# Window attention and convolution on one core: a float16 output projection, a copy moved to ScalarE, and statistics spread over more units

## Chip, cores and metric

The kernel runs on one core of a Trainium2 chip. The metric is the time of one execution on the device, in microseconds (us).

## Reference

x is 2 x 128 x 256 x 256 (two batches, 128 channels). The block computes

```
z   = groupnorm(x)                       # 32 groups of 4 channels, eps 1e-5
x1  = x + W_out . attention(z)           # windows of 8x8 queries, 12x12 keys, 4 heads of 32
y   = groupnorm(x1)
y   = y * mask(y)                        # a 32x32 tile is kept if any |value| > 1e-6
out = x1 + conv3x3(y) + bias             # 128 -> 128 channels, zero padding
```

Inside a window a query attends only to the keys whose row and column differences have one parity, so that each window falls into four independent parts of 16 queries and 36 keys. The logits are q.k plus relative logits for height and width, which come from q and two small tables. The second group norm needs the sums over all of x1 of a batch before the convolution of that batch can begin.

## The kernel before

The kernel has three stages, and each engine runs its own instruction stream in each of them; semaphores tie the streams together.

**Stage A** (to 93 us) prepares the weights and gathers the statistics of x of the first batch: VectorE runs `bn_stats` over pieces of 512 elements. A short block, `groupnorm_moments`, turns them into mean and reciprocal deviation.

**Stage B** is a loop over 128 units (`units`, written out in full), a unit being 8 image rows of half the width. `u` is the unit whose scores are computed; other steps belong to units up to 3 ahead or 3 behind. Each unit has four groups (`g`, 512 in all, `n = 4u + g`) of four windows. In a group, TensorE runs in this order: the scores of group n with the relative logits (32 small float32 products, L470), the first transposes of group n-3 (L450), the q and k projections of one part (L432, L437, three float16 products each: high x high, high weight's low half, low x high), the v projections (L484), the attention output of group n-4 (L501, into `ps_o`), the second transposes, and the output projection of a group of unit u-2 (L511, one float32 product of 256 columns into `ps_y`).

VectorE, in order: `brel` (L547), the row sum `ssum` (L551), the copy of the relative logits from `ps_s` to `rel` (L556), the reciprocal (L562), the residual addition `x1` (L571), the score addition (L580), the row maximum (L586), the spreading of q to `qb` (L600). Once a unit each come statistics of x1 (L592, g = 0), maximum and minimum over tiles (L607, g = 1 and 2). In units 6 to 37 four pieces of `bn_stats` of the second batch of x (L531) are spread over the groups.

ScalarE evicts: the transposed probabilities (L638, L656), k (L627), v (L645), the attention output to `of` (L650), then the exponential (L660), the normalisation of rows for a later unit (L684 for edge rows once a unit, L692 for own rows twice) and its float16 high half (L702). GpSimd computes `erel` (L719), the normalised probabilities `d` (L726), the products `prod` of the relative logits with a shift table (L735, waits for `rel`), the subtraction of the maximum (L742) and the low half `zl` (L749). SyncE issues all transfers; the statistics' rows (1 MB a unit, two slots) are queued in the unit that uses them, behind the rows of unit u+3.

At unit 38 the moments of the second batch of x are computed inside the loop: TensorE waits in g = 1 for VectorE's aggregate, and again for five small operations.

**Between B and C** two blocks run with nothing beside them: `groupnorm_moments("gn1", (0, 1))` for both batches of x1, and a block that turns the tile extremes into the tables `ctab` and `dtab` (scale and bias per strip and tile), with a reduction over partitions on GpSimd.

**Stage C** first writes two rows of zeros to `x1` in memory (`zrow`), loads x1 strips of 8 rows, normalises them on ScalarE (L911), combines rows on GpSimd (L984), splits into high (ScalarE, L919) and low half (VectorE, L966), multiplies on TensorE (L892) and adds on VectorE (L956), over 64 strips.

Of the kernel before, what the change touches and what calls it, by code (L numbers as in the profile page):

```python
# [5 lines left out]
F32 = mybir.dt.float32  # L6
# [74 lines left out]
def conv_preact_program(nc, x_in, wqkv_in, wout_in, rel_in, wconv_in, bias_in, ident_in, gsum_in,  # L81
                        shift_in, edge_in, own_head_in, x1_dram, out):
    with ExitStack() as ctx:
# [5 lines left out]
        wo = sb("wo", C, F32)  # L89
# [49 lines left out]
        def moments_tables(dve, link, batches, sqrt_done):  # L139
# [9 lines left out]
            for b in batches:  # L149
                link(dve.tensor_copy(mean_t[:, b * hs:(b + 1) * hs], view(moments, 0, 128, 2 * b, [[0, hs]])))  # L150
                link(dve.tensor_copy(rstd_t[:, STRIPS + b * hs:STRIPS + (b + 1) * hs],
                                     view(gn[5], 0, 128, b, [[0, hs]])))
            lo, hi = batches[0] * hs, (batches[-1] + 1) * hs
# [4 lines left out]
            for part in range(3):  # L158
                cols = slice(part * STRIPS + lo, part * STRIPS + hi)
                link(dve.scalar_tensor_tensor(shift_t[:, cols], rstd_t[:, cols], -1.0, mean_t[:, lo:hi],  # L160
                                              ALU.mult, ALU.mult))

# [45 lines left out]
        with ExitStack() as pa:  # L208
# [16 lines left out]
            with nc.Block() as block:  # L225
# [26 lines left out]
                def _(dve):  # L252
# [22 lines left out]
                    dve.tensor_copy(wo[:], rawn[:, SPANS[1][0]:SPANS[1][1]])  # L275
                    dve.tensor_copy(wq_h[:], rawn[:, 0:3 * C]).then_inc(w_qh, 1)
                    dve.wait_ge(w_qh, 1)
# [39 lines left out]
        with ExitStack() as pb:  # L317
            names = ("zf_done", "zh_done", "zl_done", "q_mm", "k_mm", "kf_done", "qb_done", "s_mm", "rel_out", "prod_done",
                     "b_done", "e_done", "s2_done", "max_done", "sub_done", "exp_done", "sum_done", "rcp_done",
                     "norm_done", "t_mm", "pt0_done", "pt1_done", "v_mm", "vf_done", "o_mm", "of_done", "y_mm",  # L320
                     "x1_done", "x1_read", "x1_stored", "zeroed", "st_used", "gn_agg_done", "gn_sum_done", "gn_step_done",
                     "gn_sqrt_done")
# [3 lines left out]
            st_loaded = [pb.enter_context(nc.semaphore(f"b_st_loaded{h}")) for h in range(2)]  # L326
            STW = WS * W
            st = sb("st", 2 * STW, F32, pb)
# [14 lines left out]
            of = sb("of", 2 * 1024, F32, pb)  # L343
# [14 lines left out]
            FIRST, LOOP = 6, 4  # L358
            STRIPS_1 = STRIPS // B
            EARLY = STRIPS_1 // LOOP  # L360
            GN = FIRST + LOOP * EARLY
            GT = UNITS * GROUPS

            GROUP_STEPS = 2 + 5

            def units(eng, body):

                some = lambda v, top: 0 <= v < top
                for u in range(-3, UNITS + 4):
                    body(u, u // 2, u % 4, some,  # L370
                         (u - FIRST, (u - FIRST) // 2) if FIRST <= u < GN else None, u == GN)

# [9 lines left out]
            def _(sp):  # L382
                def body(u, s, slot, on, stat, moments_due):
# [9 lines left out]
                    if stat is not None:  # L393

                        row = settled(sp, (stat[0] + STRIPS_1) * WS + PAD)
                        sp.wait_ge(sem["st_used"], (stat[0] + 1) * PAR)
                        sp.dma_start(st[:, h * STW:(h + 1) * STW],
                                     x_in[:, bass.ds(row, WS), :].rearrange("p a b -> p (a b)")
                                     ).then_inc(st_loaded[h], 16)
# [6 lines left out]
                    if on(u - 1, UNITS):  # L406
# [8 lines left out]
                                          UW * r:UW * r + UW]).then_inc(xr_loaded[r], 16)  # L415
                units(sp, body)
                sp.wait_ge(sem["x1_stored"], UNITS * 16)

            @block.tensor
            def _(pe):  # L420
                def project(n, p, slot, u, moments_due):
# [4 lines left out]
                    if moments_due:  # L426
                        pe.wait_ge(sem["gn_agg_done"], 1)
                        pe.matmul(ps_q[:, 0:2], gsum[:], aggr[:, 2:4], start=True, stop=True
                                  ).then_inc(sem["gn_sum_done"], 1)
                        pe.wait_ge(sem["gn_step_done"], GROUP_STEPS)  # L430
# [22 lines left out]
                def body(u, s, slot, on, stat, moments_due):  # L453
                    for g in range(GROUPS):
# [20 lines left out]
                        if on(u + ahead, UNITS):  # L475
                            project(n, (g + 1) % PAR, slot + ahead, u + ahead, moments_due and g == 1)
# [11 lines left out]
                        if on(n - 4, GT):  # L488
# [4 lines left out]
                            need(pe, sem["of_done"], m)  # L493
# [537 lines left out]
```

## Time and profile before

| | us |
|---|---|
| median of 3 runs | 3701.91 (3698.52 to 3707.66) |
| the profiled execution, its own time | 3702.19 |
| its span, first to last instruction | 3700.40 |
| PE (TensorE matmul) busy | 3491.4 |
| DVE (VectorE) busy | 3349.1 |
| ACT (ScalarE) busy | 2966.0 |
| POOL (GpSimd) busy | 2575.1 |

The span is what the trace shows; the profiled execution's own time is 1.79 us more, which lies around the first and the last instruction. A busy share over the whole span mixes three stages with different limits, so the rows below are taken by stage. Rows of the timeline give start and duration; the time from one start to the next (the step) is shorter than the duration where neighbours overlap.

### The profile page before, as it was taken

The numbers are of one execution on the slowest core, as the hardware profiler recorded it, in microseconds if no ns is written. First come the engines' busy times: TensorE is split into PE (matmuls) and PEld (weight loads), VectorE is DVE, ScalarE is ACT, GpSimd is POOL, SyncE is SP. The second block draws the span as 40 slices with busy tenths as digits, with TensorE's granted clock in tenths as the row PEclk, the third lists the DMA queues.
The fourth block names the chain that finished last, engine by engine and source line by source line (L and its number), as shares of the span: only waits on it lengthen the run. The fifth ranks groups of instructions, "written<-read, shape, count | busy, mean of one in ns | idle before, by whom it ended". The sixth has DMA issues, their size and how long they took to land. (4 is left out here: it accounts for less than half of the span.)

```text
span 3700.4 us, 127356 instructions
## 1 busy us (share of the span) xinstructions
PE 3491.4 (94%) x51718; PEld 2480.6 (67%) x51718; DVE 3349.1 (91%) x5626; ACT 2966.0 (80%) x5320; POOL 2575.1 (70%) x3344
## 2 busy tenths in 40 slices
PE   0799999998999999999999999999589999999999
PEld 0587777777888888888888888888434444444444
DVE  9699999999999999999999999999789888888887
ACT  0788888887999999999999999998377777777774
POOL 1677777776777777777777777777366666666664
PEclk9999999999999999999999999999799999999999
DMA  8244544443333333333333333333244434344332
GB/s 374 79 132 133 159 134 154 148 139 105 103 103 97 94 98 103 103 97 91 101 103 103 95 91 103 103 100 83 69 160 162 154 146 154 147 154 154 154 154 83
DMA packets 492549, 464.06 MB, mean 125 GB/s; under 512 B 9664, under 2 KB 469312, under 8 KB 469440
## 3 DMA queue, kind: packets, MB, share of 16 engines
q1 hardware_dynamic: 491968, 455.92, 38.4%
q8 instruction: 412, 6.75, 0.8%
q14 instruction: 169, 1.38, 0.1%
HBM read 321.40 MB, written 134.48 MB: 123 GB/s over the span
## 5 line engine op out<-in xcount | busy, mean ns | idle before, releaser
L984 POOL TENSOR_TENSOR sb_tf<-sb_cf 128x1024 f32<-128x1024 f32 x256 | 609.4, 2382 | 392.2 <-DVE sb_tl L966 370.3
L450 PE MATMUL ps_t<-sb_ident,sb_d 128*108 128x128 f32 x4096 | 662.3, 284 | 6.2 <-ACT sb_pt L638 1.9
L600 DVE TENSOR_TENSOR sb_qb<-ps_q,sb_own_head 128x1024 f32<-128x1024 f32 x512 | 621.1, 1213 | 14.9 <-PE ps_q L432 14.9
L470 PEld LDWEIGHTS ps_s<-sb_kf,sb_qb 128*64 128x64 f32 x16384 | 519.1, 138 | 171.5 <-issue 162.9
L719 POOL TENSOR_TENSOR sb_erel<-sb_brel 128x288 f32<-128x288 f32 x512 | 351.5, 686 | 395.6 <-DVE sb_brel L547 394.7
L892 PE MATMUL ps_c<-sb_th,sb_wc_h 128*128 128x512 f16 x1536 | 584.3, 380 | 40.3 <-DVE sb_tl L966 40.2
L470 PE MATMUL ps_s<-sb_kf,sb_qb 128*64 128x54 f32 x16384 | 585.6, 224 | 2.4 <-DVE sb_scores L580 2.4
L892 PE MATMUL ps_c<-sb_th,sb_wc_l 128*128 128x512 f16 x1536 | 583.3, 380 | 0.0
L892 PE MATMUL ps_c<-sb_tl,sb_wc_h 128*128 128x512 f16 x1536 | 583.2, 380 | 0.0
L749 POOL TENSOR_TENSOR sb_zl<-sb_zf,sb_zh 128x396 f16<-128x396 f32 x512 | 481.1, 940 | 83.1 <-ACT sb_zh L702 83.1
L735 POOL TENSOR_TENSOR sb_prod<-sb_rel,sb_shift 128x192 f32<-128x192 f32 x1024 | 502.1, 511 | 0.0
L919 ACT CAST sb_th<-sb_tf 128x1024 f16<-128x1024 f32 x256 | 263.9, 1043 | 258.9 <-POOL sb_tf L984 258.9
L450 PEld LDWEIGHTS ps_t<-sb_ident,sb_d 128*108 128x108 f32 x4096 | 410.6, 131 | 87.8 <-ACT sb_pt L638 12.1
L726 POOL TENSOR_TENSOR sb_d<-sb_scores,sb_srcp 128x288 f32<-128x288 f32 x512 | 342.6, 669 | 160.3 <-DVE sb_srcp L562 160.3
L966 DVE TENSOR_TENSOR sb_tl<-sb_tf,sb_th 128x1024 f16<-128x1024 f32 x256 | 420.0, 1641 | 20.4 <-ACT sb_th L919 20.3
L956 DVE SCALAR_TENSOR_TENSOR sb_oc<-ps_c,sb_wscale,sb_oc 128x1024 f32<-128x1024 f32 x256 | 322.6, 1281 | 86.2 <-PE ps_c L892 86.1
L911 ACT ACTIVATE sb_cf<-sb_xc,sb_dtab,sb_ctab 128x32 f32<-128x32 f32 (+2 forms) x768 | 357.2, 551 | 26.4 <-DMA sb_xc<-x 26.4
L484 PE MATMUL ps_v<-sb_wq_h,sb_zh 128*108 128x128 f16 x2048 | 369.9, 219 | 0.0
L484 PE MATMUL ps_v<-sb_wq_l,sb_zh 128*108 128x128 f16 x2048 | 369.9, 219 | 0.0
L484 PE MATMUL ps_v<-sb_wq_h,sb_zl 128*108 128x128 f16 x2048 | 369.9, 219 | 0.0
L627 ACT COPY sb_kf<-ps_k 128x576 f32<-128x576 f32 x512 | 331.6, 648 | 43.0 <-PE ps_k L437 42.7
L656 ACT COPY sb_pt<-ps_t 108x512 f32<-108x512 f32 x512 | 302.1, 590 | 75.7 <-PE ps_t L450 71.7
(117 smaller groups left out, 8228.0 us busy)
## 6 DMA issues: line engine op xcount, KB each, us to landing
sb_xb<-rows SPq DMA_DIRECT2D x128, 780.0 KB, 6.5
sb_xc<-x SPq DMA_DIRECT2D x64, 1280.0 KB, 5.4
sb_x<-rows SPq DMA_DIRECT2D x128, 512.0 KB, 4.1
x<-sb_x SPq DMA_DIRECT2D x128, 512.0 KB, 3.3
out<-sb_oc SPq DMA_DIRECT2D x64, 1024.0 KB, 3.9
sb_abuf<-rows SPq DMA_DIRECT2D x16, 2048.0 KB, 11.7
sb_st<-rows SPq DMA_DIRECT2D x32, 1024.0 KB, 9.3
sb_raw<-wconv SPq DMA_DIRECT2D x1, 576.0 KB, 3.7
```

Source lines behind the costliest of these rows:

```text
L450: last = pe.transpose(ps_t[0:KV, wj * 128:(wj + 1) * 128], d[:, at:at + KV], ident[:])
L470: last = pe.matmul(s_at, qb[:, qc:qc + QB], kf[:, kc:kc + KR], start=True, stop=True)
L484: last = pe.matmul(ps_v[0:KV, p * C:(p + 1) * C], z_at(z, vslot, p, GW * WK * vg, [[1, KV]]), w[:, 2 * C:3 * C], start=(c == 0), stop=(c = ...
L600: dve.tensor_tensor(view(qb, 0, 128, vh * QBW + p * NW * QB, [[QB, NW], [QN, HEADS], [1, QN]]), view(ps_q, 0, 128, 0, [[QN, NW], [0, HEADS ...
L719: pool.tensor_tensor(view(erel, 0, 128, 0, [[KN, PAIRS], [KS, KS], [1, KS]]), view(brel, 0, 128, 0, [[KS, PAIRS], [0, KS], [1, KS]]), view ...
L726: pool.tensor_tensor(view(d, 0, 128, b0 * DB, [[DSLOT, PAIRS], [1, KN]]), view(sp_, 0, 128, b0 * NS, [[KN, PAIRS], [1, KN]]), view(srcp, 0 ...
L735: last = pool.tensor_tensor(view(prod, 0, 128, ax * PAIRS * KS * QS, [[KS * QS, PAIRS], [QS, KS], [1, QS]]), view(rel, 0, 128, b0 * PAIRS ...
L749: pool.tensor_tensor(z_at(zl, vslot, p, 0, [[1, PLANE]]), view(zf, 0, 128, (vslot % 2) * PAR * PLANE + p * PLANE, [[1, PLANE]]), z_at(zh, ...
L892: last = pe.matmul(m_at, wt[:, tap], t_at(z), start=(c == 0), stop=(c == 8))
L911: last = act.activation(view(cf, 0, 128, c0 + off, dims), view(xc, 0, 128, r + off, dims), ACT.Identity, bias=dtab[:, col], scale=ctab[:, ...
L966: dve.tensor_tensor(view(tl, 0, 128, at, [[CW, PAIRROWS], [1, W]]), view(tf, 0, 128, k * TF, [[W, PAIRROWS], [1, W]]), view(th, 0, 128, at ...
L984: pool.tensor_tensor(tf[:, k * TF:(k + 1) * TF], view(cf, 0, 128, c0 + ra * W, [[2 * W, PAIRROWS], [1, W]]), view(cf, 0, 128, c0 + rb * W, ...
```

## The change

- The output projection takes `wo_h`, `wo_l` (float16 halves of the weight) and `oh`, `ol` (float16 halves of the attention output): three float16 products instead of one float32. ScalarE writes `oh` instead of `of`; VectorE writes `ol` = `ps_o` - `oh`, behind its residual addition of the group. TensorE's next attention output waits for `ol`.
- The copy of the relative logits moves from VectorE to ScalarE, behind the first transposed copy.
- The statistics of the second batch of x are taken in half strips (two pieces each): two half strips in each of units 0 to 3, one in each of units 4 to 59, all in g = 3. Four slots; the load is issued a unit ahead, last in SyncE's order.
- The moments of the second batch of x move from unit 38 to unit 60. The moments of x1 of the first batch are computed in the loop at unit 70, its tile extremes, the reduction and its tables at unit 71. For the second batch of x1 they move into the block of stage C, where ScalarE waits for the tables only at the strip where batch two begins. The zero rows are written in the loop.

```diff
-        wo = sb("wo", C, F32)
+        wo_h, wo_l = sb("wo_h", C, F16), sb("wo_l", C, F16)
...
+            def gathered(u):
+
+                if 0 <= u < DOUBLE:
+                    return (2 * u, 2 * u + 1)
+                return (u + DOUBLE,) if DOUBLE <= u < HALVES - DOUBLE else ()
+
+            MOMENTS = {HALVES - DOUBLE: 1, UNITS // B + 6: 0}
+            MASK = UNITS // B + 7
...
+                    for k in gathered(u + 1):
+
+                        row, r = H + k * (WS // 2) + PAD, k % ST
+                        if k >= ST:
+                            sp.wait_ge(sem["st_used"], 2 * (k - ST + 1))
+                        sp.dma_start(st[:, r * HALF:(r + 1) * HALF],
+                                     x_in[:, row:row + WS // 2, :].rearrange("p a b -> p (a b)")
+                                     ).then_inc(st_loaded[r], 16)
...
-                            need(pe, sem["of_done"], m)
+                            need(pe, sem["ol_done"], m)
...
-                            pe.matmul(ps_y[:, 0:QP], wo[:], of[:, ob * 1024 + g * QP:ob * 1024 + (g + 1) * QP],
-                                      start=True, stop=True).then_inc(sem["y_mm"], 1)
+                            for c, (o, w) in enumerate(((oh, wo_h), (oh, wo_l), (ol, wo_h))):
+                                last = pe.matmul(ps_y[:, 0:QP], w[:], o[:, ob * 1024 + g * QP:ob * 1024 + (g + 1) * QP],
+                                                 start=(c == 0), stop=(c == 2))
+                            last.then_inc(sem["y_mm"], 1)
...
-                        if on(n, GT):
-                            dve.wait_ge(sem["s_mm"], n + 1)
-                            need(dve, sem["prod_done"], n - 1)
-                            dve.tensor_copy(view(rel, 0, 128, b0 * PAIRS * 2 * RN, [[2 * RN, PAIRS], [1, 2 * RN]]),
-                                            view(ps_s[g % 2], 0, 128, KN, [[KR, PAIRS], [1, 2 * RN]])
-                                            ).then_inc(sem["rel_out"], 1)
...
+                        if on(n - 5, GT):
+
+                            v, vslot, vg = (u - 1, slot - 1, g - 1) if g else (u - 2, slot - 2, GROUPS - 1)
+                            dims = [[QP, PAR], [1, GW * QN]]
+                            dve.wait_ge(sem["oh_done"], n - 4)
+                            need(dve, sem["y_mm"], (v - 1) * PAR)
+                            dve.tensor_tensor(view(ol, 0, 128, (vslot % 2) * 1024 + vg * GW * QN, dims),
+                                              view(ps_o, 0, 128, 0, [[GW * QN, PAR], [1, GW * QN]]),
+                                              view(oh, 0, 128, (vslot % 2) * 1024 + vg * GW * QN, dims), ALU.subtract
+                                              ).then_inc(sem["ol_done"], 1)
...
+                        if g == 3:
+                            for k in gathered(u):
+                                r = k % ST
+                                dve.wait_ge(st_loaded[r], (k // ST + 1) * 16)
+                                for c in range(2):
+                                    at = UNITS * 6 + (2 * k + c) * 6
+                                    dve.bn_stats(stats[:, at:at + 6],
+                                                 st[:, r * HALF + c * 512:r * HALF + (c + 1) * 512]
+                                                 ).then_inc(sem["st_used"], 1)
+                        if u in MOMENTS:
+                            b = MOMENTS[u]
+                            if g == 0:
+                                moments_sums(dve, link[b], (b,), gn_sem[b]["agg_done"])
+                            if g == 2:
+                                moments_tables(dve, link[b], (b,), gn_sem[b]["sqrt_done"], edges=(b == 1))
+                        if u == MASK and g == 0:
+                            tile_extremes(dve, link[0], 0)
+                            dve.tensor_copy(ext[1][:, 0:1], ext[0][:, 0:1]).then_inc(sem["tiles_done"], 1)
+                        if u == MASK and g == 2:
+                            row_tables(dve, link[0], 0, sem["all_tiles"])
...
+                        if on(n, GT):
+                            act.wait_ge(sem["s_mm"], n + 1)
+                            need(act, sem["prod_done"], n - 1)
+                            act.copy(view(rel, 0, 128, b0 * PAIRS * 2 * RN, [[2 * RN, PAIRS], [1, 2 * RN]]),
+                                            view(ps_s[g % 2], 0, 128, KN, [[KR, PAIRS], [1, 2 * RN]])
+                                            ).then_inc(sem["rel_out"], 1)
...
-        groupnorm_moments("gn1", (0, 1))
...
+                    if j + 2 == CSTRIPS // B:
+                        act.wait_ge(sem["step_done"], TABLE_STEPS)
...
+                link = linker(dve, sem["step_done"])
+                moments_sums(dve, link, (1,), sem["agg_done"])
...
+                moments_group(dve, link, (1,), ps_c, sem["sum_done"])
+                moments_tables(dve, link, (1,), sem["sqrt_done"], edges=False)
+                tile_extremes(dve, link, 1)
+                dve.tensor_copy(ext[1][:, 0:1], ext[0][:, 0:1]).then_inc(sem["tiles_done"], 1)
+                row_tables(dve, link, 1, sem["all_tiles"])
```

`tile_extremes` and `row_tables` hold the work of the old block between B and C, for one batch. `row_tables` takes threshold and scale in one operation and four copies where the old block had eight scalings.

## Rows read from the trace of the kernel before

**Rows 1.** Windows: span, then busy us and instructions by engine, clock, DMA share

```profile
240.00:880.00 640.00, 619.84 (x11639) 499.71 (x11638) 619.74 (x1262) 543.24 (x1043) 481.46 (x757) 1.00 0.46 143
...
945.00:2567.00 1622.00, 1622.00 (x30923) 1331.10 (x30920) 1505.82 (x3025) 1466.81 (x2775) 1280.05 (x2016) 1.00 0.36 99
```

**Rows 2.** Timeline (start, duration) of ScalarE: edge rows, once a unit

```profile
247.98 1.48 ACT L684 ACTIVATE sb_zf<-sb_xb,sb_shift_t,sb_rstd_t 128x260 f32<-128x260 f32 x2
...
877.60 1.46 ACT L684 ACTIVATE sb_zf<-sb_xb,sb_shift_t,sb_rstd_t 128x260 f32<-128x260 f32 x2
...
945.09 1.50 ACT L684 ACTIVATE sb_zf<-sb_xb,sb_shift_t,sb_rstd_t 128x260 f32<-128x260 f32 x2
...
2566.99 1.50 ACT L684 ACTIVATE sb_zf<-sb_xb,sb_shift_t,sb_rstd_t 128x260 f32<-128x260 f32 x2
```

**Rows 3.** Waits from 240 to 860 us: total, times, longest

```profile
DVE sb_stats L531 <- DMA sb_st<-rows: 15.0, 27, 1.6
```

**Rows 4.** Timeline of TensorE's matmuls, late in the loop

```profile
1701.74 0.60 PE L511 MATMUL ps_y<-sb_of,sb_wo 128*128 128x256 f32 x2
1702.27 1.14 PE L470 MATMUL ps_s<-sb_kf,sb_qb 128*64 128x54 f32 x32
...
1703.82 0.30 PE L432 MATMUL ps_q<-sb_zh,sb_wq_h 128*128 128x256 f16 x1
...
1704.23 0.33 PE L437 MATMUL ps_k<-sb_zh,sb_wq_h 128*128 128x396 f16 x1
...
1705.35 0.22 PE L484 MATMUL ps_v<-sb_wq_h,sb_zl 128*108 128x128 f16 x1
1705.50 0.65 PE L501 MATMUL ps_o<-sb_pt,sb_vf 108*32 108x64 f32 x32
```

**Rows 5.** Timeline of VectorE: early stage, late stage, end of the loop

```profile
405.26 0.44 DVE L551 TENSOR_REDUCE sb_ssum<-sb_scores 128x8 f32<-128x288 f32 x1
405.62 0.30 DVE L556 COPY sb_rel<-ps_s 128x144 f32<-128x144 f32 x1
405.83 0.20 DVE L562 RECIPROCAL sb_srcp<-sb_ssum 128x8 f32<-128x8 f32 x1
...
409.40 0.68 DVE L531 BATCH_NORM_STATS2 sb_stats<-sb_st 128x6 f32<-128x512 f32 x1
...
1703.79 0.43 DVE L571 SCALAR_TENSOR_TENSOR sb_x<-ps_y,sb_oscale,sb_x 128x256 f32<-128x256 f32 x1
...
2625.24 0.45 DVE L551 TENSOR_REDUCE sb_ssum<-sb_scores 128x8 f32<-128x288 f32 x1 [0.76 <-ACT sb_scores L660]
2625.73 0.20 DVE L562 RECIPROCAL sb_srcp<-sb_ssum 128x8 f32<-128x8 f32 x1
```

**Rows 6.** Timeline of ScalarE: copy of the attention output

```profile
1706.22 0.37 ACT L650 COPY sb_of<-ps_o 128x256 f32<-128x256 f32 x1
```

**Rows 7.** Timeline between B and C; chain that ended last (its last three)

```profile
2646.73 7.28 DVE L118 BATCH_NORM_AGGREGATE sb_aggr<-sb_stats 128x2 f32<-128x768 f32 x2 [0.33 <-PEq L317]
...
2656.07 0.20 ACT L197 ACTIVATE sb_gn<-sb_gn 128x2 f32<-128x2 f32 x1 [8.09 <-DVE sb_gn L137]
...
2660.64 1.29 DVE L783 TENSOR_REDUCE sb_tile_ext<-sb_tmax 128x64 f32<-128x256 f32 x2 [0.56 <-PEq L180]
...
2667.60 0.23 DVE L794 TENSOR_SCALAR sb_tile_abs<-sb_tile_abs 128x128 f32<-128x128 f32 x1 [2.60 <-POOL sb_tile_abs L819]
...
2677.20 5.43 DMA sb_xc<-x
...
2682.66 6.70 ACT sb_cf L911 x16
...
2716.39 978.35 PE ps_c L892 x4518
```

**Rows 8.** Timeline of VectorE in stage C: the low half, twice

```profile
2729.43 1.30 DVE L966 TENSOR_TENSOR sb_tl<-sb_tf,sb_th 128x1024 f16<-128x1024 f32 x1
...
2760.87 2.47 DVE L966 TENSOR_TENSOR sb_tl<-sb_tf,sb_th 128x1024 f16<-128x1024 f32 x1
```

More of the change, by code:

```diff
@@ L152, in moments_tables @@
                                      view(gn[5], 0, 128, b, [[0, hs]])))
+            if not edges:
+                return
             lo, hi = batches[0] * hs, (batches[-1] + 1) * hs
@@ L161, in moments_tables, with tiles_of @@
                                               ALU.mult, ALU.mult))
+        ctab = sb("ctab", 3 * CSTRIPS * TC, F32)
+        dtab = sb("dtab", 3 * CSTRIPS * TC, F32)
+        nmean = sb("nmean", B, F32)
+        TR = ROWS // TILE
+        SPT = TILE // CROWS
+        ext = [sb(f"tile_ext{j}", TR * TC, F32) for j in range(2)]
+        tabs = sb("tile_abs", TR * TC, F32)
+        zrow = sb("zrow", W, F32)
+        def tiles_of(t, b):
+            return t[:, b * TR // B * TC:(b + 1) * TR // B * TC]
@@ new lines, in tile_extremes @@
+        def tile_extremes(dve, link, b):
+            hs, n = STRIPS // B, TR // B
+            for t, dst, op in ((tmax, ext[0], ALU.max), (tmin, ext[1], ALU.min)):
+                for h in range(2):
+                    link(dve.tensor_reduce(view(dst, 0, 128, b * n * TC + 4 * h, [[TC, n], [1, 4]]),
+                                           view(t, 0, 128, b * n * 8 * SPT + 4 * h, [[8 * SPT, n], [1, 4], [8, SPT]]),
+                                           AX.X, op))
+                part = tiles_of(dst, b)
+                link(dve.tensor_scalar(part, part, mean_t[:, b * hs:b * hs + 1],
+                                       rstd_t[:, STRIPS + b * hs:STRIPS + b * hs + 1], ALU.subtract, ALU.mult))
+            link(dve.scalar_tensor_tensor(tiles_of(ext[0], b), tiles_of(ext[1], b), -1.0, tiles_of(ext[0], b),
+                                          ALU.mult, ALU.max))
@@ L425, in project @@
                     need(pe, sem["qb_done"], piece)
[L426 to L430, printed above, removed]
+                    if due is not None:
+                        pe.wait_ge(gn_sem[due]["agg_done"], 1)
+                        pe.matmul(ps_q[:, 0:2], gsum[:], aggr[:, 2 * due:2 * due + 2], start=True, stop=True
+                                  ).then_inc(gn_sem[due]["sum_done"], 1)
+                        pe.wait_ge(gn_sem[due]["step_done"], GROUP_STEPS)
                     for c, (z, w) in enumerate(PRODUCTS):
@@ L475, in body @@
                         if on(u + ahead, UNITS):
-                            project(n, (g + 1) % PAR, slot + ahead, u + ahead, moments_due and g == 1)
+                            project(n, (g + 1) % PAR, slot + ahead, u + ahead, MOMENTS.get(u) if g == 1 else None)
                         if on(n - 3, GT):
@@ L522, in _, with body @@
                 last.then_inc(sem["zeroed"], 1)
[L523 to L535 removed]
+                link = [linker(dve, gn_sem[b]["step_done"]) for b in range(B)]
+                def body(u, s, slot, on):
                     h = slot % 2
@@ L877, in _ @@
             def _(pe):
+                pe.wait_ge(sem["agg_done"], 1)
+                pe.matmul(ps_c[:, 0:2], gsum[:], aggr[:, 2:4], start=True, stop=True).then_inc(sem["sum_done"], 1)
                 def body(j, t, slot, on):
```

186 lines of the change are left out of this document (70 added, 116 removed).

## Prediction

> **What bounds the kernel now.** I read three views in this order: the windows, the timeline of each engine, and the chain of waits at the two stage boundaries. The windows [rows 1] split the unit loop in two. From 945 us on TensorE is busy in all 1622.00 us, VectorE in 1505.82 (93%), ScalarE in 1466.81 (90%), GpSimd in 1280.05. From 240 to 880 us, while the statistics of the second batch are gathered, VectorE has 619.74 of 640 us (97%) and TensorE waits. The period of a unit is read between starts of the edge-row activation of ScalarE, one pair per unit [rows 2]: 84 periods from 945.09 to 2566.99 make 19.31 us each; 31 from 247.98 to 877.60 make 20.31. So a late unit is set by TensorE; an early one by VectorE, whose work in it is 619.74 / 640 x 20.31 = 19.67 us, and most of the rest is a wait for the statistics' rows, 15.0 us in 27 waits [rows 3], 0.48 us per unit. VectorE's work in a late unit is 1505.82 / 1622 x 19.31 = 17.93 us, ScalarE's 17.46.
>
> From 877.60 to 945.09 three units take 67.49 us, 9.56 more than three of 19.31 [rows 2]: that is the computing of one batch's moments inside the loop. Behind the loop the convolution can't begin: its first normalisation on ScalarE starts at 2682.66, while the moments block began at 2646.73 [rows 7]. From 2716.39 the end chain is TensorE alone for 978.35 us [rows 7].
>
> **The change, part by part.**
>
> *1. Output projection on TensorE.* Today one float32 product goes from 1701.74 to the start of the scores at 1702.27: 0.53 us [rows 4]. Three float16 products of the same 128x256 shape stand in the same trace as the q projection: they begin at 1703.82 and the k products follow at 1704.23, so 0.137 us each [rows 4]. What follows a float16 product with float32 weights shows at the v products: the last one starts at 1705.35, the attention product at 1705.50 [rows 4]. A 512-column product of the convolution takes 978.35 / 4518 = 0.217 us [rows 7], so 128 columns take 0.054, 256 take 0.108, and some 0.10 of the 0.15 is the turn. The new block: two steps of 0.137, then 0.108 of columns and 0.10 = 0.48. It saves 0.05 us a group, 0.21 a unit: the floor of TensorE falls from 19.31 to 19.10. Bounds: nothing saved (19.31), or no turn at all, 3 x 0.137 = 0.41, 0.12 saved (18.83). I take 0.05, put together from this engine's own steps.
>
> *2. The copy of the relative logits leaves VectorE.* Step from its start to the next instruction: 405.62 to 405.83, 0.21 us [rows 5]. But it now stands between the sum (405.26, step 0.36) and the reciprocal (405.83), which waits for that sum. Where no copy stands between them, at the loop's end, the sum starts at 2625.24 and the reciprocal at 2625.73 [rows 5]: 0.49. So 0.36 + 0.21 = 0.57 becomes 0.49: only 0.08 us is gained.
>
> *3. The low half of the attention output comes to VectorE.* 128x256, one operand from PSUM and one from SBUF. The nearest row is the residual addition of the same size and places, which lasts 0.43 us [rows 5]; neighbours overlap by 0.08 (the sum lasts 0.44 and its step is 0.36), so its step is 0.35. Bounds: 0.21, the copy's step, and the whole 0.43. I take 0.35. With part 2 that is +0.27 a group, +1.08 a unit.
>
> *4. Statistics.* Now four 512-element pieces in each of 32 units; then two in each of 56 units (units 4 to 59) and four in units 0 to 3. A piece costs its duration of 0.68 less the overlap of 0.08: 0.60 [rows 5]. So VectorE has in a unit with two pieces 19.67 - 1.20 + 1.08 = 19.55 in the figures of the early stage, and in one without pieces 19.67 - 2.40 + 1.08 = 18.35. Adding up single steps instead gives about 0.1 more, because a busy share hides short gaps; I take 19.65 and 18.45. The waits for rows go, since four slots are loaded a unit ahead. In SyncE's order these loads now come last in their unit, behind the store of x1 and the residual's rows; behind their own wait stand the rows of a unit three ahead, which have time. The two transfers of zeros join that queue once, at unit 4, at no cost. The rest of the old gap, 20.31 - 19.67 - 0.48 = 0.16 a unit, I keep as 0.14: 19.79. VectorE thus stays the bound for 56 units, 0.69 above the new floor, and is no longer it behind them.
>
> *5. The copy on ScalarE.* The copy of 256 columns from PSUM takes 0.37 us [rows 6]; 144 columns take an estimated 0.28, a step of 0.19, so 0.76 a unit: 17.46 becomes 18.2 of 19.1. The added wait, for the scores' products, is met already: the transposed copy ahead of it waits for later products of TensorE. Queued behind the copy are the k and v evictions and the attention output, and TensorE waits for those a group later; GpSimd's product waits for it too. The 0.9 us a unit that is left covers it; without that cover it would cost up to 0.76 a unit, 95 us in 125 units. TensorE's attention product of the next group now waits for the low half instead of the copy. In the late stage VectorE does that half behind the residual addition of the group, at 1703.79 + 0.35 [rows 5], so till about 1704.6, and the product comes at 1705.50 [rows 4]: it hides too. In the early stage it makes TensorE follow VectorE, which is the bound there anyway.
>
> *6. Moments of the finished x1, first batch, at unit 70.* The same code as the stall of 9.56 us, so +9.6; from zero, if covered, to 12.
>
> *7. Tile extremes and tables of the first batch at unit 71.* Both batches' extremes ran from 2660.64 to 2665.00, and the reduction over partitions added 2.60 before 2667.60 [rows 7]. Half the extremes is an estimated 2.6 us, the reduction is partly waited for, and the tables cost an estimated 2.3 (some ten operations of 0.1 to 0.5 us, as the one at 2667.60 of 0.23). With 0.6 us a unit of room on VectorE I take 5, between 0 and 10.
>
> *8. The boundary.* The new block starts at once with the second batch's moments while the rows load. The aggregate of two batches lasted 7.28 [rows 7]; one takes 3.64. The old ScalarE square root began at 2656.07, 9.34 us after the block's start; less 3.64 that is 2646.73 + 5.70, with its own 0.2 it is 2652.6, and two small fills make it 2652.9. The rows need 5.43 us from their issue, which now can be at about 2647.1 [rows 7]: 2652.5. So the normalisation starts at 2652.9 and not 2682.66: 29.8 earlier. VectorE is first needed an estimated 10 us behind it, after the first strip of 6.70 us and GpSimd's first rows [rows 7]; its own small work (tables of the moments, 2.6 of extremes, 2.6 of reduction, 2.3 of row tables) ends by my count at about 2663, just in time. I take 29; bounds 24 and 30. The 64 strips themselves don't change.
>
> *9. Setup:* one subtraction and a wait more on VectorE, +0.6.
>
> **The sum.** Loop: floor 125 units x 0.21 = -26; 56 units x 0.69 = +38.6 in place of the old early excess, 31 x 1.00 = 31 us; units 0 to 3 with their double load +2.8; the first moments stall stays; the new one +9.6; tables +5. That is -1.0. Tail of the loop an estimated -0.5, boundary -29, setup +0.6: -30. The profiled execution took 3702.19 us (span 3700.40, 1.79 around it), 0.28 above the median of 3701.91. So 3702.2 - 30 = 3672, ratio 0.992; against the median the same within a microsecond.
>
> **The rivals.**
>
> A. *Statistics spread so thin that TensorE sets the early units too.* If the low half costs 0.21 and the waits vanish, VectorE needs 19.65 - 0.56 = 19.1: -38.6, 3633. Against it: the nearest row says 0.35. Chance 0.10.
>
> B. *The float16 block saves nothing.* The turn between number formats takes back 0.05. Only the 68 or so units that TensorE sets lose: +14, 3686. Chance 0.12.
>
> C. *The copy on ScalarE delays GpSimd.* It now comes behind a transposed copy in ScalarE's order and not straight behind the scores, so GpSimd's product, its subtraction and the exponential on ScalarE form a ring with ScalarE's own work. GpSimd has 4.1 us a unit free (1280.05 of 1622.00, [rows 1]), which speaks against it. If the ring is longer than a group in one group of four by 0.2 us, 125 units lose 25: 3697. Chance 0.10.
>
> D. *The boundary gain is lost* to another wait (rows, or VectorE's small work under GpSimd's float32 work): +29, 3701. Chance 0.03.
>
> E. *Slower than before: the low half on VectorE is drawn out by GpSimd.* In the convolution the same kind of subtraction takes 1.30 us at one time and 2.47 at another [rows 8], a factor of 1.9. At 0.35 x 1.9 = 0.67 the early units cost 1.28 more (+72) and the late ones come to 19.7, 0.6 above the floor (+43): 3787. It decides from a step of about 0.48 us on: +0.13 x 4 x 56 = 29. For it speaks that GpSimd is busy in 79% of the loop [rows 1]; against it that the residual addition, which also reads PSUM and SBUF, lasts 0.43 [rows 5] beside the same GpSimd work. Chance 0.05. The Trainium skill (GPSIMD Engine Reference, Specifications) says that contention strikes VectorE instructions with two SBUF inputs or in a 2-port mode; by that rule this subtraction, with one SBUF input, is spared, and the rows agree.
>
> **How the numbers follow.** My forecast has 0.60, the rivals 0.10, 0.12, 0.10, 0.03 and 0.05. Its own range, from the bounds of parts 1, 3, 6, 7 and 8 taken together, is 3654 to 3692. The range of 3645 to 3700 leaves out A's full gain, the upper part of C, D and E. What this measurement can tell from no change is 0.3%, 11 us: faster is below 3691. Faster: 0.58 + 0.10 + 0.10 + 0.02 = 0.80. Same: 0.02 + 0.02 + 0.07 + 0.03 = 0.14. Slower: 0.06, which is E and the upper end of C.
>
> **What the profile after would show.** Period of late units 19.10 (right), 19.31 (B), more (E or C). Periods of units 4 to 59 near 19.8, VectorE without gaps; 19.1 would be A. The low half's duration: 0.43 right, above 0.56 is E. Two units with some 10 us more, at 60 and 70, and one with 5. First normalisation some 6 us behind the end of the loop. The prediction is wrong if ScalarE stops waiting for TensorE in the late stage, or if TensorE waits for the low half there.

## The result and the profile after

The changed kernel takes 3675.62 us (median of 4 runs, 3671.46 to 3676.63); the kernel before, on the same chip, 3702.09 (4 runs). The ratio is 0.9925, 95% interval 0.9911 to 0.9940: faster by 0.75%, some 4 us above the forecast of 3672. The profiled execution spans 3673.7 us, 26.7 less than before.

Windows of the changed kernel, in the columns of [rows 1] (span; busy time of TensorE, its weight loads, VectorE, ScalarE and GpSimd; granted clock, DMA share, GB/s), from an early and a late part of the loop without stalls:

```profile
240.00:880.00 640.00, 631.43 (x12184) 520.75 (x12183) 630.56 (x1246) 588.68 (x1213) 497.65 (x787) 1.00 0.42 123
1600.00:2550.00 950.00, 946.88 (x18638) 792.08 (x18640) 909.41 (x1804) 892.36 (x1855) 761.50 (x1201) 1.00 0.37 101
```

VectorE is busy in 98.5% of the early window, TensorE in 99.7% of the late one: the bounds lie where the prediction put them. The starts of the edge rows, as in [rows 2]:

```profile
112.99 1.45 ACT L768 ACTIVATE sb_zf<-sb_xb,sb_shift_t,sb_rstd_t 128x260 f32<-128x260 f32 x2
...
213.15 1.48 ACT L768 ACTIVATE sb_zf<-sb_xb,sb_shift_t,sb_rstd_t 128x260 f32<-128x260 f32 x2
...
1288.02 1.49 ACT L768 ACTIVATE sb_zf<-sb_xb,sb_shift_t,sb_rstd_t 128x260 f32<-128x260 f32 x2
1317.66 1.45 ACT L768 ACTIVATE sb_zf<-sb_xb,sb_shift_t,sb_rstd_t 128x260 f32<-128x260 f32 x2
1340.59 1.48 ACT L768 ACTIVATE sb_zf<-sb_xb,sb_shift_t,sb_rstd_t 128x260 f32<-128x260 f32 x2
...
1493.82 1.48 ACT L768 ACTIVATE sb_zf<-sb_xb,sb_shift_t,sb_rstd_t 128x260 f32<-128x260 f32 x2
1522.36 1.46 ACT L768 ACTIVATE sb_zf<-sb_xb,sb_shift_t,sb_rstd_t 128x260 f32<-128x260 f32 x2
1554.90 1.49 ACT L768 ACTIVATE sb_zf<-sb_xb,sb_shift_t,sb_rstd_t 128x260 f32<-128x260 f32 x2
...
2561.37 1.48 ACT L768 ACTIVATE sb_zf<-sb_xb,sb_shift_t,sb_rstd_t 128x260 f32<-128x260 f32 x2
```

From 213.15 to 1288.02 there are 55 periods of 19.54 us on average; the usual one is 19.52. The usual late period is 18.89. In between are two stalls: 29.64 and 22.93 (and 19.89, 18.88, 20.03 behind them) around unit 60, together 16.9 over five times 18.89; and 28.54 and 32.54 (then 19.85) at units 70 and 71, together 24.3 over three times 18.89. The forecast had 24.2 for all of them, the trace has 41.2. From the row at 112.99 to 2561.37 the loop takes 2448.38 us. Before, the same row stood here:

```profile
112.48 1.46 ACT L684 ACTIVATE sb_zf<-sb_xb,sb_shift_t,sb_rstd_t 128x260 f32<-128x260 f32 x2
```

and to 2566.99 [rows 2] it was 2454.51: -6.1.

TensorE and VectorE in a late group, answering to [rows 4] and [rows 5]:

```profile
2102.75 0.30 PE L497 MATMUL ps_q<-sb_zh,sb_wq_h 128*128 128x256 f16 x1
2102.89 0.30 PE L497 MATMUL ps_q<-sb_zh,sb_wq_l 128*128 128x256 f16 x1
...
2103.16 0.33 PE L502 MATMUL ps_k<-sb_zh,sb_wq_h 128*128 128x396 f16 x1
2103.33 0.33 PE L502 MATMUL ps_k<-sb_zh,sb_wq_l 128*128 128x396 f16 x1
...
2105.49 0.27 PE L577 MATMUL ps_y<-sb_oh,sb_wo_h 128*128 128x256 f16 x1
2105.60 0.27 PE L577 MATMUL ps_y<-sb_oh,sb_wo_l 128*128 128x256 f16 x1
2105.71 0.27 PE L577 MATMUL ps_y<-sb_ol,sb_wo_h 128*128 128x256 f16 x1
2105.92 0.27 PE L535 MATMUL ps_s<-sb_kf,sb_qb 128*64 128x54 f32 x2
```

```profile
2102.36 0.44 DVE L609 TENSOR_REDUCE sb_ssum<-sb_scores 128x8 f32<-128x288 f32 x1
2102.84 0.20 DVE L614 RECIPROCAL sb_srcp<-sb_ssum 128x8 f32<-128x8 f32 x1
2102.96 0.43 DVE L623 SCALAR_TENSOR_TENSOR sb_x<-ps_y,sb_oscale,sb_x 128x256 f32<-128x256 f32 x1
2103.31 0.42 DVE L636 TENSOR_TENSOR sb_ol<-ps_o,sb_oh 128x256 f16<-128x256 f32 x1
2103.64 0.45 DVE L643 TENSOR_TENSOR sb_scores<-ps_s,sb_erel 128x288 f32<-128x288 f32 x1
```

The projection block now takes 2105.49 to 2105.92, 0.43 us in place of 0.53. The sum stands 0.48 ahead of its reciprocal (predicted 0.49), and the low half lasts 0.42 with a step of 0.33 (predicted 0.43 and 0.35).

The timeline between the loop and the convolution, answering to [rows 7] (start, duration, engine; in brackets the idle time ahead and what ended it):

```profile
2642.13 3.62 DVE L118 BATCH_NORM_AGGREGATE sb_aggr<-sb_stats 128x2 f32<-128x768 f32 x1 [0.33 <-PEq L367]
...
2647.80 0.20 ACT L957 ACTIVATE sb_gn<-sb_gn 128x1 f32<-128x1 f32 x1 [4.41 <-DVE sb_gn L137]
2647.90 6.68 ACT L932 ACTIVATE sb_cf<-sb_xc,sb_dtab,sb_ctab 128x32 f32<-128x32 f32 x16
...
2653.02 0.55 POOL L1004 PARTITION_ALL_REDUCE sb_tile_abs<-sb_tile_ext  x1 [28.61 <-DVE sb_tile_ext L969]
...
2655.04 0.75 DVE L208 TENSOR_SCALAR sb_dtab<-sb_ctab,sb_nmean 128x768 f32<-128x768 f32 x1
2662.36 7.94 POOL L1015 TENSOR_TENSOR sb_tf<-sb_cf 128x1024 f32<-128x1024 f32 x3 [8.80 <-issue]
```

The normalisation starts 5.8 us behind the block's start at 2642.13; the forecast was 6.2 (2646.73 to 2652.9). But the first strip is complete at 2654.58, VectorE's tables at 2655.8 (13.7 behind the block's start, where 16.3 was forecast), and GpSimd's first subtraction waits until 2662.36, for nothing that the profile shows. From the block's start to the end of the last addition on VectorE the kernel takes 1027.24 us; before, 3696.05 - 2646.73 = 1049.3. That gains 22, not 29. In the kernel before, a gap behind the reduction could not show: GpSimd had nothing to do until ScalarE's first strip.

```profile
2666.77 0.72 POOL L819 PARTITION_ALL_REDUCE sb_tile_abs<-sb_tile_ext  x1 [36.85 <-issue]
2689.44 25.81 POOL L984 TENSOR_TENSOR sb_tf<-sb_cf 128x1024 f32<-128x1024 f32 x9 [21.94 <-ACT sb_cf L911]
```

The same gap stands in the loop, at unit 71 (GpSimd's timeline, then VectorE's):

```profile
1537.98 0.54 POOL L839 PARTITION_ALL_REDUCE sb_tile_abs<-sb_tile_ext  x1 [5.82 <-PE ps_t L515]
1545.45 0.68 POOL L803 TENSOR_TENSOR sb_erel<-sb_brel 128x288 f32<-128x288 f32 x1 [6.93 <-issue]
```

```profile
1546.16 0.46 DVE L643 TENSOR_TENSOR sb_scores<-ps_s,sb_erel 128x288 f32<-128x288 f32 x1 [9.82 <-POOL sb_erel L803]
```

So the difference of 26.7 is: setup +0.5, loop -6.1, its tail +1.0, behind the loop -22.1.

### The profile page after: what moved, and what is told of

Read it like the earlier page. It is cut to its first block and busy times, and to the rows that moved or that the text cites. A ratio compares the mean times of both kernels' runs of the same rounds, so it can differ in the third digit from the quotient of the medians.

```text
span 3673.7 us, 129440 instructions
## 1 busy us (share of the span) xinstructions
PE 3461.0 (94%) x52232; PEld 2490.3 (68%) x52232; DVE 3399.8 (93%) x5647; ACT 3035.0 (83%) x5835; POOL 2570.7 (70%) x3345
## 5 line engine op out<-in xcount | busy, mean ns | idle before, releaser
L566 PE MATMUL ps_o<-sb_pt,sb_vf 108*32 108x64 f32 x16384 | 339.6, 222 | 29.6 <-DVE sb_ol L636 13.9
```

The source lines that it names most:

```text
L566: last = pe.matmul(o_at, v_at, p_at, start=True, stop=True)
```

## The experiments

All times are medians against the kernel before, run on the same chip; in brackets the ratio to it and its 95% interval. "Period" is the time between the starts of the edge rows. "Theory 1" is the first explanation that an expectation names. The code shown is cut down to what matters.

**One part alone, and one undone.** First the float16 projection and its low half put into the kernel before, nothing else:

```diff
-pe.matmul(ps_y[:, 0:QP], wo[:], of[...], start=True, stop=True)
+for c, (o, w) in enumerate(((oh, wo_h), (oh, wo_l), (ol, wo_h))):
+    last = pe.matmul(ps_y[:, 0:QP], w[:], o[...], start=(c == 0), stop=(c == 2))
+dve.tensor_tensor(ol[...], ps_o[...], oh[...], ALU.subtract)   # behind the residual addition
```

> The kernel before with the float16 projection and its low half on VectorE alone. Theory 1 (the step costs VectorE 0.33 a group and TensorE gains 0.10): a late unit has 17.93 + 4 x 0.33 = 19.25 us of VectorE work against a TensorE floor of 18.89, so VectorE sets it at about 19.3, no gain over 19.31; the 32 units with statistics go from 20.31 to 21.6, +42. Sum: 3745 us, slower by 1.2%. Rival (TensorE's gain of 0.42 a unit reaches the time, since neighbours on VectorE overlap more when it is pressed): late units 19.0, 90 x -0.3 = -27, sum about 3717.

Measured: 3700.42 us (0.9993, 0.9983 to 1.0002). Late units fall to 18.88, though VectorE carries both the copy and the low half; units with four pieces of statistics rise from 20.31 to 21.04. My sum of 19.25 for a late unit was too high, and with it both forecasts, 3745 and the rival's 3717: it added a step of 0.33 to a busy share of 17.93. From 2000 to 2370 us VectorE is busy in 98.7% of the time (365.20 of 370) and TensorE in all of it, so it is still TensorE that sets these units, as the rival had it. 84 late periods gain 33 us, 31 early ones lose 25 and the stall 2: nearly nothing is left.

The copy of the relative logits moved alone:

```diff
-dve.tensor_copy(view(rel, ...), view(ps_s[g % 2], ...))      # between sum and reciprocal
+act.copy(view(rel, ...), view(ps_s[g % 2], ...))             # behind the transposed copy
```

> The kernel before with the copy of the relative logits on ScalarE alone. Theory 1 (VectorE gains only 0.08 us a group, because the reciprocal must then wait for its own sum): units with statistics 20.31 - 0.3 = 20.0, 32 x -0.3 = -10; late units stay 19.31. Sum 3692 us. Rival (the whole step of 0.21 is gained): -27, 3675. Rival (GpSimd is delayed by the copy's place behind ScalarE's transposed copy): late units above 19.31, time at or above 3702.

Measured: 3699.6 us (0.9992, 0.9982 to 1.0002). 29 periods from unit 8 average 20.05 in place of 20.34, late ones are 19.31 as before. GpSimd does not lengthen a unit. The early periods bear theory 1 out (0.29 gained, 0.3 forecast). The time gained 3 us of the 10 forecast: 0.08% can't be told from no change.

The statistics spread alone, with the boundary left as it was:

```diff
-if stat is not None: stat_pieces(stat, h, (0, 4, 1, 2)[g], (1, 0, 1, 2)[g])   # units 6 to 37
+if g == 3:
+    for k in gathered(u): ...                                # two pieces a unit, units 4 to 59
```

> The kernel before with the statistics spread over 60 units and loaded a unit ahead, the moments at unit 60, and nothing else. Theory 1 (VectorE's work per unit is what set the early units): 17.93 + 1.20 = 19.13, under TensorE's 19.31, so all units take 19.31 and the 31 us of the old early excess go: 3671 us, as low as the whole change. Rival (part of the excess was the short order around the pieces, which stays): early units at 19.5, 56 x 0.2 = 11 more, 3682.

Measured: 3672.35 us (0.9914, 0.9898 to 0.9931), the same as the whole change. Its periods are 19.31 from unit 5 to the end, but for one stall of 28.73 (and 18.78 behind it).

The changed kernel with its float32 projection back:

```diff
-for c, (o, w) in enumerate(((oh, wo_h), (oh, wo_l), (ol, wo_h))): ...
-dve.tensor_tensor(ol[...], ps_o[...], oh[...], ALU.subtract)
+pe.matmul(ps_y[:, 0:QP], wo[:], of[...], start=True, stop=True)
```

> The changed kernel with the float32 projection put back and no low half on VectorE. Theory 1: late units 19.31 again in place of 18.89, 68 x 0.42 = +29; early units 19.31 in place of 19.52, 56 x -0.21 = -12; the first stall falls from 16.9 to about 10, since the attention product no longer waits for VectorE: -7. Sum 3686 us, 0.3% above the changed kernel. Rival (the late gain of 0.42 came from the copy that left VectorE and not from the block of products): late units stay 18.9, early 18.9, time about 3650.

Measured: 3671.2 us (0.9912, 0.9896 to 0.9929). All units take 19.31; the stalls at 60 and 70 cost 8.27 each and the one at 71 12.8. So late units follow the block of products, as theory 1 has it, but its sum of 3686 is 15 us too high. Outside the stalls 57 late periods make 24 us, less 4.5 in odd ones of the changed kernel, where I had 29; the early units and the stalls give back 24 where I had 19. Inside the whole change the float16 projection is worth nothing that can be measured (the intervals of 0.9912 and 0.9925 overlap).

The changed kernel with the copy back on VectorE:

```diff
-act.copy(view(rel, ...), view(ps_s[g % 2], ...))
+dve.tensor_copy(view(rel, ...), view(ps_s[g % 2], ...))      # between sum and reciprocal
```

> The changed kernel with the copy of the relative logits back on VectorE. Theory 1 (its place between the sum and the reciprocal makes it cost only 0.07 to 0.08 us there): early units 19.52 + 0.3 = 19.8, 56 x 0.3 = +17; late units stay 18.89; 3692 us. Rival (it costs its whole step of 0.21): early units 20.36, +47, 3723, and late units above 18.89.

Measured: 3688.03 us (0.9965, 0.9951 to 0.9979). Early units take 19.85, 0.33 more or 0.08 a group; late ones 18.89. Where VectorE is the bound the copy costs what stood in the prediction.

**What bounds an early unit.** The statistics of the second batch left out, its moments taken from other columns:

```diff
 def gathered(u):
-    if 0 <= u < DOUBLE: ...
+    return ()
```

> The changed kernel without loading and gathering the second batch's statistics in the loop; its moments are worked out from other columns, so the second batch's values are wrong by that. Theory 1 (two pieces of statistics a unit are what holds the early units at 19.52): all early units at 18.89, 56 x -0.63 = -35, and 3641 us. Rival (TensorE's wait for the low half holds them, with or without statistics): early units stay above 19.2, over 3655.

Measured: 3635.39 us (0.9817, 0.9800 to 0.9833): early units at 18.89.

The two pieces of a unit in groups 1 and 3:

```diff
-if g == 3: both pieces of the unit
+return ((u + DOUBLE, g // 2),) if g in (1, 3) and ... else ()   # one piece in a group
```

> The changed kernel with the two statistics pieces of a unit in two groups (1 and 3) and not both in group 3; nothing else. Theory 1 (the sum of VectorE's work in a unit sets the early units, 98.5% of 19.52): at most the idle 0.29 goes, 19.25 to 19.5, between -15 and 0: 3661 to 3676 us. Rival (the two pieces in one group of 4.7 us are what TensorE waits for, and the sum is not the bound): early units at 18.9 to 19.1, 3645 us.

Measured: 3675.28 us (0.9925, 0.9908 to 0.9942), early units at 19.51 to 19.52. The place of the pieces changes nothing; the sum of VectorE's work is the bound, and the last 1.5% of the window is no room here. The periods of the kernels bound by VectorE also give the prices: four pieces, copy and low half 21.04; two pieces, 19.85; two without the copy, 19.52. A piece is thus (21.04 - 19.85) / 2 = 0.595, and an early unit without pieces would ask 19.52 - 1.19 = 18.33 of VectorE, under TensorE's 18.89.

**The reduction over partitions.** A plain copy in its place leaves out the maximum over channels:

```diff
-pool.partition_all_reduce(tiles_of(tabs, b), tiles_of(ext[0], b), 128, RMAX)
+pool.tensor_copy(tiles_of(tabs, b), tiles_of(ext[0], b))
```

> The changed kernel with both reductions over partitions on GpSimd replaced by a plain GpSimd copy of the same tile; it leaves out the maximum over channels. Theory 1 (after a reduction GpSimd takes some 7 to 9 us before its next instruction, and that gap, not the reduction's own 0.55 us, holds up the loop at unit 71 and the start of the convolution): unit 71 falls from 32.5 by about 8, to 24 or 25; the first GpSimd subtraction of the convolution comes straight behind the first normalised strip, about 7 us earlier. Sum 3676 - 15 = 3661 us. Rival (VectorE's own small work sets both places): both stay, at most -1 each, 3674.

Measured: 3656.97 us (0.9878, 0.9862 to 0.9895), 18.6 less than the changed kernel and 4 under theory 1. Unit 71 falls from 32.54 to 22.75, and from the block's start to the end it is 1019.34 us in place of 1027.24. GpSimd's timeline at both places:

```profile
1533.13 0.24 POOL L839 COPY sb_tile_abs<-sb_tile_ext 128x64 f32<-128x64 f32 x1 [2.47 <-DVE sb_tile_ext L690]
1533.61 0.69 POOL L803 TENSOR_TENSOR sb_erel<-sb_brel 128x288 f32<-128x288 f32 x1 [0.24 <-DVE sb_brel L605]
...
2641.76 0.24 POOL L1004 COPY sb_tile_abs<-sb_tile_ext 128x64 f32<-128x64 f32 x1 [28.66 <-DVE sb_tile_ext L969]
2643.50 8.12 POOL L1015 TENSOR_TENSOR sb_tf<-sb_cf 128x1024 f32<-128x1024 f32 x3 [1.50 <-ACT sb_cf L932]
```

Behind a copy the next instruction follows at once, or with the strip that it waits for. The gap belongs to the reduction.

**Versions built on this.** The maximum over channels serves only to tell whether any channel exceeds a threshold. A 0/1 map multiplied by a matrix of ones says the same, exactly, on TensorE:

```diff
+dve.tensor_scalar(ext1, ext0, THRESHOLD, None, ALU.is_gt)
+pe.matmul(ps_q[:, QP:QP + TN], ones[:], ext1, start=True, stop=True)
+dve.tensor_scalar(tabs, ps_q[:, QP:QP + TN], 0.5, rstd, ALU.is_gt, ALU.mult)  # ahead of the eviction of q
+if g in SLOTS(u): steps.emit(dve, 1)       # one queued small instruction a unit, from 66 on
```

> The changed kernel, whole computation, with the first batch's moments and tables not done in two units but one small VectorE instruction in each unit from 66 to 123, TensorE reading and writing a free part of the query accumulator, the maximum over channels taken as a product of a 0/1 map with ones on TensorE (so no GpSimd reduction), and seven eighths of the second aggregate ahead of the boundary. Theory 1: the stalls at units 70 and 71 (9.7 + 13.7 = 23.4) go but for 1 or 2, and the convolution starts 7 earlier: 3676 - 22 - 7 = 3647 us. Rival (VectorE has no room in a late unit, and the same work costs the same spread thin): some 18 us of it come back, 3665.

Measured: 3641.15 us (0.9831, 0.9815 to 0.9847). The edge rows at units 68 to 72, where the changed kernel has its second pair of stalls:

```profile
1470.43 1.48 ACT L889 ACTIVATE sb_zf<-sb_xb,sb_shift_t,sb_rstd_t 128x260 f32<-128x260 f32 x2
...
1545.95 1.49 ACT L889 ACTIVATE sb_zf<-sb_xb,sb_shift_t,sb_rstd_t 128x260 f32<-128x260 f32 x2
```

18.88 in all four periods: the same work, one instruction a unit, fits into VectorE's spare time. From the block's start to the end it is 1019.97, -7.3, as with the plain copy:

```profile
2624.92 0.69 PE L1014 MATMUL ps_c<-sb_tile_ext,sb_ones 128*128 128x64 f32 x2 [6.20 <-DVE sb_tile_ext L257]
2625.65 0.28 DVE L267 TENSOR_SCALAR sb_tile_abs<-ps_c,sb_rstd_t 128x64 f32<-128x64 f32 x1 [0.78 <-PE ps_c L1014]
...
2629.87 7.93 POOL L1133 TENSOR_TENSOR sb_tf<-sb_cf 128x1024 f32<-128x1024 f32 x3 [30.71 <-ACT sb_cf L1052]
```

Then each projection where its engine has room:

```diff
+terms = ((oh, wo_h), (oh, wo_l), (ol, wo_h)) if u - 2 >= 42 else ((of, wo),)
+GATHER = {0: (0, 1), ..., 4: (8,), 5: (9, 10), ...}          # three pieces a unit, done at unit 41
```

> The kernel e8_thin_tables with the float32 projection in the first 42 strips' units, where statistics are gathered three pieces a unit, and the float16 projection from unit 42 on; both batches' moments spread thin. Theory 1 (VectorE sets a unit that has both statistics and the low half; TensorE sets all others): units 4 to 42 at 19.31, units 44 to 127 at 18.89, no stall at 60, 70 or 71: the loop is 2380 us long in place of 2448, with the boundary 3676 - 68 - 7 = 3601 us. Rival (three pieces a unit are too many beside the float32 projection): units 4 to 42 at 19.7, 3617. Rival (the low half costs the same in late units once the small work is added): late units at 19.0 to 19.1, 3615.

Measured: 3608.61 us (0.9748, 0.9731 to 0.9764), the best of all, 2.5% under the kernel before. Edge rows:

```profile
210.37 1.49 ACT L899 ACTIVATE sb_zf<-sb_xb,sb_shift_t,sb_rstd_t 128x260 f32<-128x260 f32 x2
...
866.95 1.49 ACT L899 ACTIVATE sb_zf<-sb_xb,sb_shift_t,sb_rstd_t 128x260 f32<-128x260 f32 x2
...
2501.29 1.49 ACT L899 ACTIVATE sb_zf<-sb_xb,sb_shift_t,sb_rstd_t 128x260 f32<-128x260 f32 x2
```

34 early periods of 19.31; behind unit 60 the usual one is 18.88. From unit 43 to 58, with two small instructions a unit, it is 19.06. There, from 1180 to 1260 us, VectorE is busy in 78.83 of 80 us and TensorE in 79.64. I take it that VectorE's room is used up; no run tests it. These units make 3 of the 7.6 us over the forecast, and odd periods the rest.

Two attempts to bring the early units to 18.9 as well:

```diff
-dve.tensor_reduce(brel, prod[..., 4], AX.X, ALU.add)
+pool.tensor_tensor(halfsum, prod[..., 0:2], prod[..., 2:4], ALU.add)   # units 0 to 42
+pool.tensor_tensor(brel, halfsum[..., 0], halfsum[..., 1], ALU.add)
```

> The kernel e9_mixed with the float16 projection in all units, and in the first 43 units the sum over four neighbours of the relative products done by two additions on GpSimd in place of VectorE's reduction; the computation is whole. Theory 1 (GpSimd has the room: 15.1 us a unit and an estimated 3.1 more, under 18.89; VectorE falls to an estimated 18.3): all units at 18.9, 39 x -0.42 = -16 against e9_mixed, 3592 us. Rival (the longer chain on GpSimd, from ScalarE's copy to the scores, becomes the bound of a group): early units at 19.5 or more, 3616 us or above.

Measured: 3620.42 us (0.9780, 0.9764 to 0.9797). The periods alternate, 18.96 with two pieces and 19.74 with four in group 3; 30 from unit 8 average 19.40. From 240 to 880 us TensorE waits 16 times for the low half, 12.5 us in all, and VectorE 90 times for GpSimd's `erel`, 25.1 us. Theory 1's 3592 is missed by 28, and the time is the rival's (3616 or above).

```diff
-at = pieces of whole halves, all in group 3
+at = divmod(q, 4) if q < 16 else ((q - 16) // 3 + 4, (q - 16) % 3 + 1)   # unit, group of piece q
```

> The kernel e10_pool_sums with one statistics piece in each of the groups 1, 2 and 3 of units 4 to 41, in place of two or four pieces in group 3. Theory 1 (the alternation of 18.96 and 19.74 there comes from the four pieces in one group): all early units at 18.95 to 19.05, 38 x -0.35 = -13, 3607 us, the same as e9_mixed within 0.1%. Rival (GpSimd, busy in 95% of these units, holds them at 19.3): 3619 us.

Measured: 3617.74 us (0.9770, 0.9754 to 0.9786). The alternation is gone, most early periods are 19.05 to 19.20, but several reach 19.6 to 20.9, and 30 periods from unit 8 average 19.35. The place of the pieces explains the alternation: TensorE's waits for the low half fall to 2.4 us. The time is that of the rival, in which GpSimd holds the early units (3619). GpSimd is busy in 610.05 of 640 us there, and VectorE waits 63 times for its `erel`, 21.5 us in all, a wait that the changed kernel's early window does not have; TensorE's waits without a cause in the profile are 6.8 us. No run separates the two, so what holds these units above 18.9 stays open. Both lose to e9_mixed.

## Why the prediction was right, and where it was off

The likeliest case came true, with the time inside its own range and 4 us above it; that closeness owes something to errors of opposite sign.

*1, the projection.* The saving is 0.10 to 0.11 a group, close to the 0.12 of the bound that I had called "no turn at all", and the floor is 18.89, not 19.10. The cost behind the last product is there, though: 2105.71 to 2105.92, 0.21, as I had put it (0.108 + 0.10). What was wrong is the step: I took 0.137 from the products of q, whose moving operand is read in pieces of four, and those still step by 0.14 in the trace after; the ones of the projection, with contiguous columns, step by 0.11. The products of k, contiguous too, step by 0.17 for 396 columns, the same 0.43 ns a column, against 0.54 for q. No run changed the layout of one product alone. 60 late units x 0.21 = -13 us against the forecast.

*2 and 3, the copy and the low half.* Both right: 0.08 a group (e11_rel_back) and a step of 0.33.

*4, the early units.* The mechanism is right (e7_no_stats, e12_apart), and the piece costs 0.595 where 0.60 was predicted. The size was 19.52, not 19.79: my addition in the figures of the busy share gave 19.55, and I then laid 0.10 for "single steps" and 0.14 for an old gap on top. Neither exists once the rows come in time. 55 x -0.27 = -15 us.

*5, the copy on ScalarE,* hides: the late units take 18.89 with it (changed kernel) and without (e11_rel_back), early ones gain. GpSimd waits for it often (114.5 us in 152 waits from 1600 to 2550 us), at no cost to the period. Neither sign by which the prediction would have been wrong is there: in that window ScalarE still waits for TensorE's transposes (35.7 us in 106 waits), and TensorE never for the low half.

*6, the moments.* The second stall, at unit 70, is 28.54 - 18.89 = 9.65, as predicted. The first was taken as unchanged and is 16.9. A wait that did not exist before stands in TensorE's timeline:

```profile
1321.52 1.08 PE L566 MATMUL ps_o<-sb_pt,sb_vf 108*32 108x64 f32 x32 [2.75 <-DVE sb_ol L636]
```

The attention product waits for the low half, which is queued behind the tables; the change had made VectorE a step on TensorE's path. Over the same five periods the stall is 8.3 us without the low half (e4_f32_proj) and 8.9 in e3_spread_alone; with it, 11.1 (e11_rel_back), 11.7 (e8_thin_tables), 13.2 without statistics (e7_no_stats), 14.4 (e12_apart), 15.4 (e5_pool_copy) and 16.9. So the low half costs some 3 us, about the length of its wait. Part of the rest goes with TensorE's granted clock. e8_thin_tables gives the engines the same loop instructions up to here and has the same wait, but not the fall of the clock behind it (windows from this attention product to the next one, first of the changed kernel, then of e8_thin_tables with its wait):

```profile
1321.52:1328.88 7.36, 7.36 (x93) 6.02 (x94) 6.35 (x13) 4.33 (x8) 4.55 (x8) 0.59 0.30 85
```

```profile
1320.35 0.65 PE L655 MATMUL ps_o<-sb_pt,sb_vf 108*32 108x64 f32 x32 [2.88 <-DVE sb_ol L749]
...
1320.35:1325.07 4.72, 4.72 (x93) 3.95 (x93) 4.59 (x11) 3.82 (x8) 3.80 (x7) 1.00 0.15 40
```

The same 93 matmuls take 7.36 us in the changed kernel, where the clock is at its lower level from 1322 to 1325.5 us (0.50, 1.2 GHz; the attention product lasts 1.08 and not 0.65), and 4.72 in e8_thin_tables. That is 2.6 of the 5.2 us between the two stalls. Why the clock falls behind the one wait and not behind the other is open. The prediction looked at this wait only in undisturbed groups.

*7, the tables at unit 71:* 13.7, not 5, outside the bound of 10. Some 9.8 of it go with the reduction (32.54 to 22.75, e5_pool_copy). I had priced the reduction by what VectorE waited for it, 2.60 [rows 7], and never asked when GpSimd takes its next instruction.

*8, the boundary:* the normalisation came as forecast; the step that failed is "VectorE is first needed an estimated 10 us behind it". It is GpSimd that comes late. The missing 7 us are its gap: 7.9 come back with the plain copy, 7.3 with the product of ones.

*9, setup:* +0.5 for +0.6. The tail lost 1.0 where 0.5 less was forecast.

*The sum of the loop:* forecast -1.0; -15 (early), -13 (late), +17 (stalls), and some +6 in odd periods of up to 20.5 make the measured -6.

*The range.* The prediction's own 3654 to 3692 does not follow from its bounds laid end to end: those of parts 1 and 3 alone reach 18 and 31 us below the forecast. How it was put together is not said.

*The rivals.* A fell by its own price, the low half at 0.33; by the prices above TensorE would have set the early units only below 0.17 a group. B, C and E are excluded by the periods of 18.89, and E also by the 0.42 of the low half beside a busy GpSimd. D was a quarter true, by a mechanism that it did not name.

What the prediction missed as a whole is how the parts trade: spread statistics alone give 30 us (e3_spread_alone), the boundary 22, and moments and tables moved into a loop whose VectorE had just been filled take half of that away.

## What to carry to other kernels

Where two engines take turns as the bound over the stages of a loop, choose a variant per stage: the float32 form where VectorE is full, the float16 form where TensorE is. Small chained work costs its whole length when it is put into one iteration, and nothing that shows when it goes in one instruction a unit, with its waits postponed to the next one, where the engine has the room. And price an instruction by when its own engine goes on, not by how long its reader waited.

## What the hardware showed unexpectedly

A reduction over partitions on GpSimd is recorded with 0.54 and 0.55 us, but GpSimd's next instruction began 6.93 us behind it in the loop and 8.80 at the boundary, with nothing to wait for; with a plain copy in its place (0.24) this gap is absent. With the copy the kernel is 18.6 us of 3676 faster. The profile doesn't say what GpSimd does in the gap.

VectorE, busy in 98.5% of a window by the records, had no room left: moving its pieces changed no period (19.52), while at 95.7% (late window) one small instruction a unit was free. The share alone does not tell which engine sets the pace: in the late units of e1_f16_alone VectorE is busy in 98.7% and TensorE sets the period.

Float16 products with contiguous moving columns step by 0.11 us for 256 columns, those with pieces of four by 0.14; nothing else was varied to show that the pieces are the cause.

Late in the loop TensorE shows single waits of 0.4 to 1.7 us for nothing in the profile, some in pairs of units some 39 us apart (in the changed kernel at 1866.86 and 1905.89), at much the same units in several kernels; the kernel before and e3_spread_alone have none late in the loop. Their cause was not tried.
